# Mamba block between two feed-forward layers: the carry of the scan moves to ScalarE, the sum of squares to VectorE, and the scan is divided 24 to 40

## The reference, cut to what matters

```python
def step(h, inp):
    dA_t, dB_t, x_t, C_t, t = inp
    h = h * dA_t + dB_t * x_t[:, :, None]
    nrm = jnp.sqrt(jnp.sum(h * h, axis=(1, 2), keepdims=True))
    fac = jnp.minimum(20.0 / (nrm + 1e-08), 1.0)
    h = jnp.where(t % 10 == 0, h * fac, h)
    y = jnp.einsum('bdn,bn->bd', h, C_t) + D_param * x_t
    return (h, y)
```

## Time and profile before

| what | value |
|---|---|
| time, median of 3 runs | 1534.88 us (1534.82 to 1535.24) |
| profiled execution, own time | 1534.2 us |
| its span | 1532.4 us |
| busy TensorE / VectorE / ScalarE / GpSimd | 1446.3 / 1253.5 / 1119.2 / 941.0 us |
| first and last carry of the scan stage | 428.4 and 1317.3 us |
| second scan half, clamp, first scan half (mean) | 0.88, 0.13, 0.88 us |
| weighing L1119 (mean) | 1445 ns, 410 times |
| mean granted TensorE clock | 0.991 |

### The profile page before, as it was taken

How to read it: one execution, slowest core, us unless ns; L and a number is a source line. 1 busy time by engine, 2 the same in 40 slices (tenths; PEclk the granted TensorE clock), 3 DMA queues, 4 the chain that set the end, 5 groups by cost and what they waited for, 6 DMA issues and landing times.

```text
span 1532.4 us, 25717 instructions
## 1 busy us (share of the span) xinstructions
PE 1446.3 (94%) x7022; PEld 1019.1 (67%) x7022; DVE 1253.5 (82%) x2526; ACT 1119.2 (73%) x2618; POOL 941.0 (61%) x956
## 2 busy tenths in 40 slices
PE   6999999999879999999999999999999998999998
PEld 5555555555467777777777777777666666677776
DVE  7776566745479999999999999999999999788884
ACT  4454455445999999999999999999999964334243
POOL 0224323432269999999999999999999998400000
PEclk9999999999999999999999999999999999999999
DMA  8224427444747666666657666566544347465520
GB/s 269 83 70 155 145 95 198 134 163 128 240 133 208 170 165 189 168 171 167 171 158 187 181 162 180 157 175 169 137 110 110 98 102 234 121 218 186 157 77 28
DMA packets 232326, 236.30 MB, mean 154 GB/s; under 512 B 46296, under 2 KB 198040, under 8 KB 232184
## 3 DMA queue, kind: packets, MB, share of 16 engines
q1 hardware_dynamic: 231240, 233.34, 52.9%
q10 hardware_dynamic: 944, 1.31, 0.2%
HBM read 136.31 MB, written 98.56 MB: 153 GB/s over the span
## 4 chain that ended last, share of the span: by engine, by line
DVE 35%; POOL 14%; PE 12%; issue 5%; DVEq 1%; POOLq 1%; DMA 1%; ACT 0%; SPq 0%; ACTq 0%
DVE h L1344 22%; POOL rc L1108 13%; DVE banks L1334 9%; PE banks L1493 4%; PE banks L1514 3%; PE banks L1524 3%; DVE qs L1328 2%; PE banks L1168 1%; DVEq L1342 1%; DMA ub<-scratch_ub 1%; DVE q_ln_st L1770 1%; DVE q_g L1679 1%; POOLq L1116 1%; DVE q_x L1651 1%; PE banks L1534 0%
## 5 line engine op out<-in xcount | busy, mean ns | idle before, releaser
L1344 DVE TENSOR_TENSOR_SCAN h<-decay,banks 128x352 f32<-128x352 f32 x820 | 710.4, 881 | 57.2 <-DVE banks L1334 2.9
L1119 POOL TENSOR_TENSOR hc<-h,bc 128x640 f32<-128x640 f32 x410 | 592.5, 1445 | 0.0
L1168 PE MATMUL banks<-hc,w_ident 128*128 128x320 f32 (+1 forms) x1664 | 525.7, 439 | 0.1
L1237 ACT ACTIVATE tb<-dtc,a 128x320 f32<-128x320 f32 (+1 forms) x832 | 417.5, 556 | 4.8 <-DVE x L611 4.8
L1168 PEld LDWEIGHTS banks<-hc,w_ident 128*128 128x128 f32 x1664 | 284.5, 191 | 70.2 <-issue 0.4
L1259 ACT ACTIVATE decay<-tb 128x640 f32<-128x640 f32 x410 | 295.2, 724 | 0.0
L1108 POOL TENSOR_TENSOR rc<-qs,w_mhalf 128x1 f32<-128x1 f32 x410 | 224.9, 549 | 107.0 <-DVE qs L1328 107.0
L1154 PE MATMUL banks<-ub 128*128 128x176 f32 x1640 | 272.2, 288 | 2.1 <-DMA ub<-scratch_ub 2.0
L1147 PEld LDWEIGHTS banks<-sc_ss,sc_ones 128*128 128x128 f32 x820 | 123.3, 189 | 158.1 <-ACT sc_sq L1248 151.3
L1154 PEld LDWEIGHTS banks<-ub 128*128 128x128 f32 x1640 | 216.4, 192 | 2.4 <-DMA ub<-scratch_ub 2.3
L1147 PE MATMUL banks<-sc_ss,sc_ones 128*128 128x1 f32 x820 | 151.6, 254 | 37.7 <-ACT sc_sq L1248 19.0
(11 more groups left out here) (133 smaller groups left out, 1812.5 us busy)
## 6 DMA issues: line engine op xcount, KB each, us to landing
ub<-scratch_ub SPq DMA_DIRECT2D x410, 107.5 KB
bc<-scratch_blk SPq DMA_DIRECT2D x205, 160.0 KB, 3.5
scratch_ub<-turned SPq DMA_DIRECT2D x64, 512.0 KB, 3.5
scratch_ub<-spread SPq DMA_DIRECT2D x64, 176.0 KB, 2.4
scratch_xc<-xc SPq DMA_DIRECT2D x8, 1024.0 KB, 4.8
scratch_sg<-sg SPq DMA_DIRECT2D x8, 1024.0 KB, 5.8
piece<-scratch_u SPq DMA_DIRECT2D x32, 256.0 KB, 4.0
q_ys<-scratch_y SPq DMA_DIRECT2D x8, 1024.0 KB, 5.6
```

The costliest lines, as they stand in the source:

```text
L1119: pool.tensor_tensor(hc[:, pl % 2, :, at * S:(at + 1) * S] .rearrange("p (c b n) e -> p c b n e", c=KE, b=B)[:, :, b], state(m)[:, :, 0:S] ...
L1168: mm = pe.matmul(banks[:, y_bank(p), 0:KE * B * wide], w.ident[:], rhs, start=(n == 0), stop=(n == N - 1))
L1237: act.activation(tanh_rows(c, r), dtc[:, c % 2, k * B:(k + 1) * B, 0:blocks_of(c) * S].rearrange("p b (k e) -> p k b e", e=S), ACT.Tanh, s ...
L1344: dve.tensor_tensor_scan(state(m).rearrange("p r e -> p (r e)")[:, half], decay[:, m % DRING, half], psI[m % B][:, half], 0.0, ALU.mult, A ...
```

## The change

The carry becomes an instruction of ScalarE, a copy with a scale, one unit ahead of the scan in ScalarE's order. The squares become an instruction of VectorE, a scalar_tensor_tensor that computes (h x 1.0) x h and writes the sum along the row as well; it stands behind the second part of the scan. The scan's two parts hold 24 and 40 rows instead of 32 and 32. TensorE's `inputs` waits for both parts within its first two instructions. The squares of the states before the first unit move out of the first stage into the start of VectorE's scan function.

```diff
@@ first stage, ScalarE
         scan.tanhs(act, 0, 33, 52)
-        scan.squares(act, 0)
-        scan.squares(act, 1)
         softplus(LAST, 0, KE)
@@ scan_stage
+    FIRST_ROWS = 24
     HR = NCH // 2
+    split = [slice(0, FIRST_ROWS * W), slice(FIRST_ROWS * W, NCH * W)]
@@ TensorE, inputs(m)
-                if m >= B and c % (KE // 2) == 0:
-                    pe.wait_ge(h_ready[c // (KE // 2)], m + 1)
+                if m >= B and c < 2:
+                    pe.wait_ge(h_ready[c], m + 1)
@@ squares
-    def squares(act, m):
+    def squares(dve, m):
         b = m % B
+        last = state(m - B)[:, :, S]
         for x in range(2):
-            act.wait_ge(h_ready[x], m + 1)
+            dve.wait_ge(h_ready[x], m + 1)
         if m >= B:
-            act.wait_ge(sum_ready, m - B + 1)
-        act.activation(sq[:, b, :], state(m - B)[:, :, S], ACT.Square,
-                       accum_out=ss[:, b:b + 1]).then_inc(sq_ready, 1)
+            dve.wait_ge(sum_ready, m - B + 1)
+        dve.scalar_tensor_tensor(out=sq[:, b, :], in0=last, scalar=1.0, in1=last, op0=ALU.mult, op1=ALU.mult,
+                                 accum_out=ss[:, b:b + 1]).then_inc(sq_ready, 1)
@@ ScalarE
+        def carry(m):
+            b = m % B
+            act.wait_ge(norm_ready, m + 1)
+            act.wait_ge(inp_ready, m + 1)
+            act.activation(inp(m)[:, :, 0], state(m - B)[:, :, S], ACT.Copy, scale=rc[:, b:b + 1]
+                           ).then_inc(carry_ready, 1)
...
+        carry(0)
         for m in range(UNITS):
...
-            if m + B < UNITS:
-                squares(act, m + B)
+            if m + 1 < UNITS:
+                carry(m + 1)
@@ VectorE
-        def carry(m):
-            b = m % B
-            dve.wait_ge(norm_ready, m + 1)
-            dve.wait_ge(inp_ready, m + 1)
-            dve.tensor_scalar(inp(m)[:, :, 0], state(m - B)[:, :, S], rc[:, b:b + 1], None, ALU.mult
-                              ).then_inc(carry_ready, 1)
...
-            half = slice(x * HR * W, (x + 1) * HR * W)
-            dve.tensor_tensor_scan(state(m).rearrange("p r e -> p (r e)")[:, half], decay[:, m % DRING, half],
-                                   psI[m % B][:, half], 0.0, ALU.mult, ALU.add).then_inc(h_ready[x], 1)
+            part = split[x]
+            dve.tensor_tensor_scan(state(m).rearrange("p r e -> p (r e)")[:, part], decay[:, m % DRING, part],
+                                   psI[m % B][:, part], 0.0, ALU.mult, ALU.add).then_inc(h_ready[x], 1)
...
+        squares(dve, 0)
+        squares(dve, 1)
         dve.wait_ge(zeroed, 1)
...
         for m in range(UNITS):
-            carry(m)
             scan(m, 0)
             if B <= m + 1 < UNITS:
                 clamp(m + 1)
             scan(m, 1)
+            if m + B < UNITS:
+                squares(dve, m + B)
```

More of the change, by code:

```diff
@@ L727 @@
 Scan = namedtuple("Scan", """sync gpsimd tensor scalar vector load_first load_units tanhs decay_rates decay_scale masks
-    decay_ready y_out y_copied squares load_piece turn_piece high_piece low_piece store_piece ut_lo
+    decay_ready y_out y_copied load_piece turn_piece high_piece low_piece store_piece ut_lo
     spread_b store_b copy_bt b_split""")
@@ L1379, in scan_stage @@
     return Scan(sync, gpsimd, tensor, scalar, vector, load_first, load_units, tanhs, decay_rates, decay_scale, masks,
-                decay_ready, y_out, y_copied, squares, load_piece, turn_piece, high_piece, low_piece,
+                decay_ready, y_out, y_copied, load_piece, turn_piece, high_piece, low_piece,
                 store_piece, ut_lo, spread_b, store_b, copy_bt, b_split)
```

## The result

The changed kernel takes 1843.5 us (four runs, 1837.5 to 1844.8) against 1535.1 us for the kernel before on the same chip (1534.8 to 1536.2): 1.200 times as long, 95% interval 1.197 to 1.203. The profiled execution took 1844.8 us, its span is 1843.0 us.

What follows compares the result with a forecast made beforehand. It took a loop of VectorE's carry, scan and clamp with GpSimd's power, 2.13 us a unit, as the bound. Changed units of 2.99: 409 x 2.99 + 7 = 1230, +341 on 1534.2 gives 1875 us, range 1790 to 1940.

Steps and rivals of the forecast that it cites:

- one loop, through the power: Scan stretch before the change: VectorE's carry, first scan half and clamp, then GpSimd's power L1108, 2.13 us a unit.
- The squares wait for the end of the weighing: VectorE's squares, two SBUF inputs, stand until GpSimd's L1119 (1.45 us) ends; costs some 1.1 us a unit, chance 0.84.
- The terms of a unit: Scan to clamp 0.62, to power 0.28, to weighing 0.52, weighing 1.45, squares 0.10, to next scan 0.02: 2.99 us.
- what is left after L1119: VectorE's squares once GpSimd's weighing ends: 0.10 us taken, from 0.09 to 0.20, then 0.02 to the next scan.
- the lower end (-0.08): Squares to next scan on VectorE: -0.08 us if the scan starts before the squares' record ends; up to +0.19, taken +0.02.
- The late units: Scan units in which something else came late: 18 us before the change, of which 7 us were kept.
- The 7: Us kept for four L1637 and four gate operations on VectorE, 0.6 net each; other delays vanish under longer units.
- The cover: Carry on ScalarE, 0.32 us: costs nothing if VectorE needs it after 1.95 us; VectorE was said to need it much later.
- What is covered: ScalarE's queue of 2.16 us lies inside the 2.99 unit; TensorE's total needs 0.48 and has 0.62, less up to 0.08.
- The weighing lets the squares through: Rival: squares run beside GpSimd's weighing, VectorE's queue sets a unit of 2.05 us, time 1493 us; chance 0.08.
- Half rate: Rival: VectorE's squares and GpSimd's weighing share SBUF reads at half rate, unit 2.41 us, time 1641 us; chance 0.06.
- ScalarE takes the place: Rival: port costs nothing, carry queues behind ScalarE's 2.16 us of work, unit 2.13 to 2.16, 1535 or more; chance 0.02.

## Why the prediction was right, point by point

**What bounds the kernel before.** Right only in part. The prediction named one loop, through the power. Shortened by 0.18 (the division alone), it bought 0.03 a unit; VectorE's own queue and the loop through ScalarE's squares are nearly as long (both about 2.1 with 24 and 40 rows). The forecast for the changed kernel did not hang on this, since the wait for the weighing makes the unit longer than all of them.

**The squares wait for the end of the weighing.** Right, and the cause is shown from several sides: one input moved out of SBUF takes the wait away; a shorter GpSimd instruction shortens it; an earlier or later start changes the duration and not the end. The rows of the first stage had told it on other lines: nine L644 begin inside an L1002, with which they share no tensor, and all end 0.55 behind it. The trace of before held no case on the line itself. The Trainium skill's page "SBUF — State Buffer", section "SBUF: two separate sides", has an exclusive hold for the whole instruction; this agrees with the 0.12 to 0.13 between the two ends in the changed kernel and with 32 and 16 rows, and it does not agree with the 214 squares beside the power. The measurement decides: no hold lasts through the power's 0.55 us. What is shown is that the wait hangs on where the squares' inputs lie and on a product of GpSimd being under way. What inside the chip holds the instruction, and whether the power lets it through for its single column or for its kind, no run shows.

One number on the way was misread: 787 ns is the minimum of L1002, its median is 826, which makes 2.35 ns a column and not 2.24. Nothing in the sum hangs on it.

**The terms of a unit.** Predicted 0.62 + 0.28 + 0.52 + 1.45 + 0.10 + 0.02; measured 0.62 + 0.27 + 0.51 + 1.45 + 0.05 for the last two together. The step that was mis-sized is "what is left after L1119". The squares' record ends 0.12 behind the weighing, but the scan does not wait for that: it starts 0.07 before, beside the 77 ns accumulator read. I had the lower end (-0.08) from the earlier trace rows and chose a value nearer to the middle. Unit 2.90 instead of 2.99: 409 x 0.09 = 37 us too many. The late units cost 10 instead of 7 (1196.1 - 409 x 2.90), and the stages outside the carries took 648.7 us instead of the 645.3 I kept. -37 + 3 + 3 = -31, from 1875 to 1844.

The 7 was not worked out to the end: eight operations at 0.6 are 5, and the eight late units at the end of the scan did take 3.50 each, 0.6 more. Not all the others vanished. Eight units between 445 and 474 us took 0.2 to 1.0 more: in each the clamp waits for TensorE's total and comes 0.76 to 1.53 behind the scan instead of 0.62. Two short units at the ends of the scan take back about 2.

Of the last 3, nearly all is the first carry, which came 2.9 later (431.3 for 428.4); the prediction did not price it. The trace shows why: the first power ends at 427.98 (428.21 before), but the first carry now stands in ScalarE's queue behind the four exponentials that run ahead (428.81 to 431.43). Before, the first scan waited for one of them only; now it starts 2.0 later (431.79 for 429.82).

**The division.** The scan paid 2.05 ns a column as worked out: 693 and 1054 ns for the forecast 0.70 and 1.06, and the clamp at 0.62.

**The carry.** 377 ns on ScalarE instead of 0.32; it ends at 905.85, over 1 us before the scan needs it, so its size did not count. The cover was named rightly: taken away (carry back on VectorE) it costs 186.

**What is covered.** ScalarE's queue stayed inside the unit, as forecast, and so did the total but for the units between 445 and 474 us. TensorE's share of the span fell to 80%.

**The rivals.** "The weighing lets the squares through" did not happen, but its price was close: with the wait removed the kernel took 1507 where the rival said 1493. About half of the units took 2.01, less than that rival's 2.05; most of those in which ScalarE also has a copy to do took 2.11 to 2.18, and 2.43 with two copies, which its sum left out. The mean is 2.10. "Half rate" has fallen. Nor is there a sign that the instruction by itself runs slower with two inputs in SBUF: with no weighing beside it, it takes 276 ns, and 267 with one of them in PSUM, where half rate would add some 67 (64 columns at the prediction's 1.042 ns). "ScalarE takes the place" did not happen in the changed kernel. Only with both steps on ScalarE does that engine fill up, and then the kernel takes 63 more than that rival's 1535.

## What to carry to other kernels

Before an operation moves to VectorE, count its SBUF inputs and look at what GpSimd is running at that moment: here two inputs beside a long GpSimd product cost the rest of that product, and the summary shows that rest as busy time; beside a one-column power they cost nothing. One operand in PSUM took the wait away, and a GpSimd instruction cut in two took most of it. Where shortening one step of a loop gives less than its size, look for a second loop of nearly the same length before cutting further.

## What the runs showed of the hardware that was not expected

- GpSimd's power did not hold the squares (268 to 292 ns beside it), though both its operands are in SBUF, while its products L1119 and L1002 held them until their end.
- The accumulated sum of a VectorE instruction is an instruction of its own in the trace (77 ns). No delay of the next one beyond 0.01 is to be seen: the scan's record starts together with it (904.00), 0.07 before that of the squares ends, much as the second scan half of the kernel before starts 0.08 before the clamp's record ends.
- ScalarE's scaled copy of 64 strided values into PSUM (377 ns) takes longer than its square of the same 64 values in SBUF (314 ns).
- A clamp that had to wait for the total takes 0.16 us where one that found it ready takes 0.13.
